# A Mamba-and-router layer on one core: conv halo on GpSimd, carries of two slots in one copy, router and last norm in other slots

## The chip, the core and the metric

The kernel runs on one NeuronCore of a Trainium2 chip. The metric is device time in microseconds (us) of one execution; every kernel has an interval from several. The engines are TensorE (PE; its weight loads are PEld), VectorE (DVE), ScalarE (ACT), GpSimd (POOL) and SyncE (SP), which issues every DMA.

## What is computed

Two blocks in a row on `x` of 2 x 2048 tokens, 512 wide, all float32. The first is a Mamba block, the second a router with an expert bias:

```python
x_in = resid_norm @ W_in                          # 1024 channels
conv = depthwise_conv(x_in, conv_w, taps=4)        # causal, along the tokens
x = silu(conv + conv_b)
delta = softplus(x @ W_delta_1 @ W_delta_2 + b_delta_2)
Bm, Cm = x @ W_B, x @ W_C                          # 16 states
h = h * exp(delta * A) + (delta * x) * Bm          # along the tokens, 1024 channels x 16 states
y = sum over states of h * Cm;  y = (y + x * W_D) * silu(skip)
x1 = x0 + layernorm(resid + y @ W_out)
scores = softmax(layernorm(x1) @ router_w + router_b)
out = x1 + layernorm(flat * sum(top8) + top8 @ expert_bias)
```

## The kernel before

The 4096 tokens are 16 chunks of 256 (`T`). A software pipeline runs in **steps** of one chunk each, and a step has 32 **slots** (`SLOTS`). The scan is the backbone: in each slot VectorE runs two `TENSOR_TENSOR_SCAN` instructions of 512 tokens (`scan`, L950), for one state and two tiles of 128 channels. Around it stand:

- ScalarE: `decay` (L707) makes exp(delta * A) for the next slot, and in a **turned** slot `make_ut` (L726) makes the scan's input transposed.
- TensorE: `turn_u` (L1124) transposes that input into the PSUM tile `bank`; it needs the scan of the slot before, since `bank` has one place for each of the two scans. `add_y` (L1129) adds h * C of two slots ago to `y_sum`.
- GpSimd: `weigh` (L612) makes h * C (`hc`) of the slot before. In the ten **plain** slots (`PLAIN_SLOTS`) `make_u` (L596) makes the scan's input for two slots on, and ScalarE writes the exponential to `bank`.

Each engine has its program written out by hand: for step and slot, first the scan's work, then what the jobs of neighbouring chunks have at that slot. The jobs are `norm` (chunk i+3), `prep` (i+2: projection, convolution, delta, B, C), `scan` (i), `gate`, `mix` (i-2: skip, output projection) and `route` (i-3: second norm, router, last norm, output). `at(step, slot)` gives each job its own slot number `s`, which runs on into the next step, so s = 40 of `route` is slot 8 of the step after. `due` returns a semaphore value to wait for, or nothing where an earlier wait covers it.

What the change touches, all on VectorE unless said:

- The convolution (L1008), for each pair `p` of channel tiles in the slots `TAPPED[p]` and `TAPPED[p] + 2`, one tile each. ScalarE has written the last tap with the bias to `hv`. VectorE adds the halo to the first 3 columns, then three taps of 253, 254 and 255 columns. Between these it makes the halo for the next chunk: three instructions on 3, 2 and 1 columns into `edge`. Tap and halo instructions alternate, so each halo instruction stands where its tap waits for the one before (`link`).
- `save_carry` (L921): a copy of the last column of the slot's two scans, after the scans of the next slot.
- `route`: the row maximum `nmx` (L1072, s = 32), the top 8 (L1082 to L1089, s = 34), `o` (L1098, s = 38 and 40), and `moments(o)` (L925 and L928, s = 40). POOL makes the scale of the last norm at s = 42 and the sum x1 + o (L683) at s = 45. SP stores `o` at s = 47, in its single queue of DMAs.

```python
                                    if s in (TAPPED[p], TAPPED[p] + 2):
...
                                        for k in range(TAPS - 1):
                                            reach = TAPS - 1 - k
                                            part = halo[:, 0:reach]
                                            done = weighed(part, got[:, T - reach:], k, part if k else bias_over(reach))
                                            if k == TAPS - 2:
                                                done.then_inc(edge_ready.sem, 1)
                                            last = weighed(row[:, reach:], got[:, 0:T - reach], k, row[:, reach:])
```

## Time and profile before

| | |
|---|---|
| median of 3 executions | 2269.61 us (2267.01 to 2277.3) |
| the profiled execution | 2263.58 us, its span 2261.6 us |
| busy: PE, DVE, ACT, POOL | 85%, 79%, 76%, 81% of the span |
| TensorE's granted clock, mean | 0.953 of full speed |

The span counts from the first instruction to the last. Scans start at 120.6 us and end at 2108.6 us; in between are 16 steps. The first three take 116 to 125 us, the eleven after them 127 to 131 us each, and the rest is the pipeline's filling and draining. "Busy" is the time in which an engine runs an instruction, waits left out. A step that the text below calls "the shown step" is the one whose first scan starts at 1120.7 us and whose successor's starts at 1248.6 us.

### The profile page before, as it was taken

The numbers are of one execution on the slowest core, as the hardware profiler recorded it, in microseconds if no ns is written. First come the engines' busy times: TensorE is split into PE (matmuls) and PEld (weight loads), VectorE is DVE, ScalarE is ACT, GpSimd is POOL, SyncE is SP. The second block draws the span as 40 slices with busy tenths as digits, with TensorE's granted clock in tenths as the row PEclk, the third lists the DMA queues.
The fourth block names the chain that finished last, engine by engine and source line by source line (L and its number), as shares of the span: only waits on it lengthen the run. The fifth ranks groups of instructions, "written<-read, shape, count | busy, mean of one in ns | idle before, by whom it ended". The sixth has DMA issues, their size and how long they took to land. (4 is left out here: it accounts for less than half of the span.)

```text
span 2261.6 us, 36229 instructions
## 1 busy us (share of the span) xinstructions
PE 1914.7 (85%) x12005; PEld 1602.1 (71%) x12005; DVE 1796.8 (79%) x3105; ACT 1716.9 (76%) x3404; POOL 1840.5 (81%) x1160
## 2 busy tenths in 40 slices
PE   5677777988889898898989898898989989888883
PEld 4567676868778687877778686877768686767551
DVE  3478878798898988898888888889888988888422
ACT  2479797887879796987879797887979788888321
POOL 1278889797989898998979898898989899999412
PEclk9889899999999999999999999999999999999996
DMA  5556566665747576665747566564757556554320
GB/s 162 186 183 201 171 188 223 211 221 174 228 144 268 174 226 203 220 206 173 234 157 263 168 200 235 194 226 147 246 173 241 170 164 231 179 182 159 118 69 19
DMA packets 234676, 425.96 MB, mean 188 GB/s; under 512 B 18622, under 2 KB 134906, under 8 KB 234490
## 3 DMA queue, kind: packets, MB, share of 16 engines
q1 hardware_dynamic: 234490, 423.65, 57.6%
q8 instruction: 96, 1.57, 0.3%
q14 instruction: 90, 0.74, 0.1%
HBM read 339.18 MB, written 84.41 MB: 187 GB/s over the span
## 5 line engine op out<-in xcount | busy, mean ns | idle before, releaser
L612 POOL TENSOR_TENSOR hc<-h,c_all 128x1024 f32<-128x1024 f32 x512 | 1206.1, 2367 | 183.9 <-DVE h L950 169.8
L950 DVE TENSOR_TENSOR_SCAN h<-operand,carry,bank 128x512 f32<-128x512 f32 x528 | 658.7, 1272 | 152.1 <-PE bank L1124 121.4
L726 ACT ACTIVATE u_t<-dx_t,lbc 128x256 f32<-128x256 f32 x1408 | 632.2, 498 | 62.7 <-PE bank L1124 62.7
L1124 PE MATMUL bank<-ident,u_t 128*128 128x128 f32 x2816 | 450.4, 285 | 228.4 <-DVE h L950 214.7
L1129 PE MATMUL y_sum<-ident,hc 128*128 128x128 f32 x4096 | 604.4, 279 | 4.7 <-POOL hc L612 4.3
L1124 PEld LDWEIGHTS bank<-ident,u_t 128*128 128x128 f32 x2816 | 343.0, 146 | 367.7 <-issue 241.4
L1129 PEld LDWEIGHTS y_sum<-ident,hc 128*128 128x128 f32 x4096 | 494.2, 145 | 47.6 <-issue 36.0
L707 ACT ACTIVATE operand<-delta_q,neg_a 128x512 f32<-128x512 f32 x704 | 479.8, 711 | 0.0
L707 ACT ACTIVATE bank<-delta_q,neg_a 128x512 f32<-128x512 f32 x320 | 218.5, 683 | 260.4 <-DVE h L950 259.8
L596 POOL TENSOR_TENSOR operand<-dx_q,b_all 128x1024 f32<-128x1024 f32 x160 | 378.8, 2367 | 8.7 <-DMA b_all<-bc_dram 8.4
L950 DVE TENSOR_TENSOR_SCAN h<-bank,carry,operand 128x512 f32<-128x512 f32 x240 | 294.9, 1269 | 11.8 <-POOL operand L596 7.4
L1335 PE MATMUL mixed<-wout,ys 128*128 128x512 f32 x512 | 264.3, 605 | 3.5 <-DVE ys L1044 3.5
L1255 PE MATMUL pair_bank<-rnt,win 128*128 128x256 f32 x1024 | 251.3, 392 | 11.9 <-DVE x L988 8.4
L950 DVE TENSOR_TENSOR_SCAN h<-operand,bank 128x512 f32<-128x512 f32 x176 | 210.3, 1213 | 59.4 <-PE bank L1124 44.8
L1309 PE MATMUL routed<-rnt_gate,wskip 128*128 128x256 f32 x1024 | 245.5, 385 | 11.2 <-DVE thg L1032 8.7
L1255 PEld LDWEIGHTS pair_bank<-rnt,win 128*128 128x128 f32 x1024 | 195.2, 198 | 49.2 <-issue 21.5
L1309 PEld LDWEIGHTS routed<-rnt_gate,wskip 128*128 128x128 f32 x1024 | 190.2, 193 | 36.7 <-issue 9.8
L1008 DVE SCALAR_TENSOR_TENSOR hv<-pair_bank,taps,hv 128x253 f32<-128x253 f32 (+2 forms) x384 | 181.5, 473 | 0.0
L646 POOL TENSOR_TENSOR dx<-delta,x 128x1024 f32<-128x1024 f32 x32 | 75.8, 2371 | 61.0 <-ACT delta L817 61.0
L1335 PEld LDWEIGHTS mixed<-wout,ys 128*128 128x128 f32 x512 | 79.3, 192 | 36.9 <-issue 32.8
L950 DVE TENSOR_TENSOR_SCAN h<-bank,operand 128x512 f32<-128x512 f32 x80 | 94.1, 1210 | 9.0 <-ACT bank L707 7.3
L1266 PE MATMUL pair_bank<-wlbc,x 128*128 128x160 f32 x512 | 92.2, 330 | 6.7 <-DVE x L988 6.7
(115 smaller groups left out, 1963.6 us busy)
## 6 DMA issues: line engine op xcount, KB each, us to landing
c_all<-bc_dram SPq DMA_DIRECT2D x256, 512.0 KB, 4.3
b_all<-bc_dram SPq DMA_DIRECT2D x160, 256.0 KB, 5.5
win<-in_L_attn_W_in SPq DMA_DIRECT2D x64, 512.0 KB, 5.7
wskip<-in_L_attn_W_skip SPq DMA_DIRECT2D x64, 512.0 KB, 6.7
x_dram<-x SPq DMA_DIRECT2D x64, 256.0 KB, 6.3
delta_dram<-delta SPq DMA_DIRECT2D x32, 512.0 KB, 7.5
dx_dram<-dx SPq DMA_DIRECT2D x32, 512.0 KB, 5.4
delta_q<-delta_dram SPq DMA_DIRECT2D x32, 512.0 KB, 6.6
```

The lines of the kernel that those rows point to most:

```text
L596: nc.gpsimd.tensor_tensor(operand[:, number % 3], dx_q[:, k], b_all[:, j % 2:j % 2 + 1].to_broadcast([P, 2, SPAN]), ALU.mult).then_inc(u_r ...
L612: nc.gpsimd.tensor_tensor(hc[:, number % 3], h[:, number % 3], c_all[:, j % 2, s % 2:s % 2 + 1].to_broadcast([P, 2, SPAN]), ALU.mult).then ...
L707: nc.scalar.activation(to, delta_q[:, k, q], ACT.Exp, scale=neg_a[:, et, n:n + 1]).then_inc(exp_ready.sem, 1)
L726: last = nc.scalar.activation(u_t[:, j % 2, b], dx_t[:, k, b], ACT.Copy, scale=lbc[:, stage % 2, b, DELTA + n:DELTA + n + 1])
L950: nc.vector.tensor_tensor_scan(h[:, number % 3, q], first, second, start, ALU.mult, ALU.add).then_inc(scan_done.sem, 1)
L1008: return nc.vector.scalar_tensor_tensor(out=to, in0=of, scalar=taps[:, et, k:k + 1], in1=onto, op0=ALU.mult, op1=ALU.add)
L1124: last = transpose(bank[:, q, b * P:(b + 1) * P], u_t[:, j % 2, b, q * P:(q + 1) * P], ident[:])
L1129: return matmul(to, lhsT=of, rhs=ident[:], is_transpose=True, start=start, stop=stop, skip_group_check=True)
L1255: last = matmul(pair_bank(p)[:, e * T:(e + 1) * T], win[:, p % 2, k, e * P:(e + 1) * P], rnt[:, k, :], start=(k == 0), stop=(k == KD - 1))
L1266: last = matmul(pair_banks[0][:, b * LBC:(b + 1) * LBC], x[:, et, b * P:(b + 1) * P], wlbc[:, et, :], start=(et == 0 and b == 0), stop=(et ...
L1309: last = matmul(routed[:, e * T:(e + 1) * T], wskip[:, p % 2, k, e * P:(e + 1) * P], rnt_gate[:, k, :], start=(k == 0), stop=(k == KD - 1))
L1335: last = matmul(mixed[:], ys[:, et, b * P:(b + 1) * P], wout[:, et, :], start=(et == 0), stop=(et == ET - 1))
```

## The change

It does five things:

- VectorE no longer makes the halo. At the second tile of a pair it copies the last three inputs of both tiles to `tail` (one instruction, `tail_ready`). At s = 21 of `prep` GpSimd makes the halo of all 8 tiles in six instructions, each linked to the one before (`edge_ready`, now once a chunk).
- `save_carries` runs in even slots only and copies the carries of two slots in one instruction; the tile `carry` is laid out so that it can.
- The second tile's taps have slots of their own, `TAPPED_NEXT`: pair 1 goes from slot 3 to slot 2.
- `route` moves: nmx from s = 32 to 33, exp and top 8 from 34 to 35, the transposition of the weights from 35 (late in the slot) to 36 (early), the bias matmuls from 37 and 39 (late) to 38 and 40 (early), `o` from 38 and 40 to 39 and 41, `moments(o)` from 40 to 43, POOL's scale from 42 to 45, ScalarE's norm from 44 to 47, POOL's sum from 45 to 48 and SP's store from 47 to 50.
- Slot 16 is plain in place of slot 18.

```diff
-PLAIN_SLOTS = (0, 2, 4, 7, 10, 13, 18, 22, 25, 29)
+PLAIN_SLOTS = (0, 2, 4, 7, 10, 13, 16, 22, 25, 29)
 TAPPED = (-5, 1, 6, 10)
+TAPPED_NEXT = (-3, 2, 8, 12)
...
-        carry = sb("carry", P, N, ET)
+        carry = sb("carry", P, N // 2, 2, ET)
...
-                            if "route" in jobs_now and s == 47:
+                            if "route" in jobs_now and s == 50:
...
+                                if s == 21:
+                                    if v := due(pool, tail_ready, t, PAIRS):
+                                        pool.wait_ge(tail_ready.sem, v)
+                                    if v := due(pool, conv_done, t, ET):
+                                        pool.wait_ge(conv_done.sem, v)
+                                    width = TAPS - 1
...
+                                    link(times(edge[:], tail[:], tap(0, width)))
+                                    link(nc.gpsimd.tensor_tensor(edge[:], edge[:],
+                                                                 cbias[:].unsqueeze(2).to_broadcast([P, ET, width]),
+                                                                 ALU.add))
+                                    link(times(tail[:, :, 0:1], tail[:, :, 2:3], tap(2, 1)))
+                                    link(times(tail[:, :, 1:3], tail[:, :, 1:3], tap(1, 2)))
+                                    link(nc.gpsimd.tensor_tensor(edge[:, :, 0:2], edge[:, :, 0:2], tail[:, :, 1:3],
+                                                                 ALU.add))
+                                    last = nc.gpsimd.tensor_tensor(edge[:, :, 0:1], edge[:, :, 0:1], tail[:, :, 0:1],
+                                                                   ALU.add)
+                                    last.then_inc(edge_ready.sem, 1)
...
-                    if v := due(dve, carry_saved, t, s - 1):
+                    if v := due(dve, carry_saved, t, (s - 1) // 2):
...
-                    if v := due(dve, scan_done, t, 2 * (s + 1)):
+                    if v := due(dve, scan_done, t, 2 * (s + 2)):
                         dve.wait_ge(scan_done.sem, v)
-                    copied(carry[:, n, 2 * quarter:2 * quarter + 2],
-                           h[:, number % 3, :, SPAN - 1]).then_inc(carry_saved.sem, 1)
+                    first = number % 3
+                    both = h[:, 0:3:2] if first == 2 else h[:, first:first + 2]
+                    copied(carry[:, n // 2, :, 2 * quarter:2 * quarter + 2],
+                           both[:, :, :, SPAN - 1]).then_inc(carry_saved.sem, 1)
...
-                        save_carry(step, slot - 1)
+                        if slot % 2 == 0:
+                            save_carries(step, slot - 2)
...
-                                    if s in (TAPPED[p], TAPPED[p] + 2):
+                                    if s in (TAPPED[p], TAPPED_NEXT[p]):
...
+                                        if e:
+                                            pair = pair_bank(p).rearrange("p (e t) -> p e t", e=2)
+                                            copied(tail[:, 2 * p:2 * p + 2], pair[:, :, T - width:]).then_inc(
+                                                tail_ready.sem, 1)
                                         for k in range(TAPS - 1):
                                             reach = TAPS - 1 - k
-                                            part = halo[:, 0:reach]
-                                            done = weighed(part, got[:, T - reach:], k, part if k else bias_over(reach))
-                                            if k == TAPS - 2:
-                                                done.then_inc(edge_ready.sem, 1)
...
-                                if s == 32:
+                                if s == 33:
...
-                                if s in (38, 40):
-                                    b = (s - 38) // 2
+                                if s in (39, 41):
+                                    b = (s - 39) // 2
...
-                                if s == 40:
+                                if s == 43:
                                     if v := due(dve, o_ready, t, TB):
                                         dve.wait_ge(o_ready.sem, v)
                                     moments(o, mvo, var_o)
```

VectorE's order in slot 8 of a full step, before (line L950 is the two scans of a slot, L1008 the taps and the halo):

```order
L950 SCALAR_TENSOR_TENSOR h<-operand,carry,bank 128x512 x2
L921 TENSOR_REDUCE carry<-h 128x2
L1098 SCALAR_TENSOR_TENSOR o<-h,stats,routed 128x512
L925 BN_STATS stat<-o 128x6 x2
L928 BN_AGGR mvo<-stat 128x2 x2
L1008 SCALAR_TENSOR_TENSOR hv<-pair_bank,taps,edge 128x3
L1008 SCALAR_TENSOR_TENSOR edge<-pair_bank,taps,cbias 128x3
L1008 SCALAR_TENSOR_TENSOR hv<-pair_bank,taps,hv 128x253
L1008 SCALAR_TENSOR_TENSOR edge<-pair_bank,taps,edge 128x2
L1008 SCALAR_TENSOR_TENSOR hv<-pair_bank,taps,hv 128x254
L1008 SCALAR_TENSOR_TENSOR edge<-pair_bank,taps,edge 128x1
L1008 SCALAR_TENSOR_TENSOR hv<-pair_bank,taps,hv 128x255
```

Slot 8 and slot 9 of the same step now (L972 is the scans, L1035 the taps, L1127 is `o`):

```order
L972 SCALAR_TENSOR_TENSOR h<-operand,carry,bank 128x512 x2
L943 TENSOR_REDUCE carry<-h 128x2x2
L1035 SCALAR_TENSOR_TENSOR hv<-pair_bank,taps,edge 128x3
L943 TENSOR_REDUCE tail<-pair_bank 128x6
L1035 SCALAR_TENSOR_TENSOR hv<-pair_bank,taps,hv 128x253
L1035 SCALAR_TENSOR_TENSOR hv<-pair_bank,taps,hv 128x254
L1035 SCALAR_TENSOR_TENSOR hv<-pair_bank,taps,hv 128x255
L972 SCALAR_TENSOR_TENSOR h<-operand,carry,bank 128x512 x2
L1082 TENSOR_TENSOR z<-mixed,z 128x512
L1127 SCALAR_TENSOR_TENSOR o<-h,stats,routed 128x512
```

The halo's three instructions and the moments of `o` have left slot 8, and the second half of `o` now stands in slot 9 behind `z`.

GpSimd's order from slot 20 to slot 22, before:

```order
L596 TENSOR_TENSOR operand<-dx_q,b_all 128x1024
L612 TENSOR_TENSOR hc<-h,c_all 128x1024 x2
L646 TENSOR_TENSOR dx<-delta,x 128x1024
L574 TENSOR_SCALAR stats<-mvh 128x2
L575 TENSOR_TENSOR stats<-stats,mhalf 128x2
```

and now:

```order
L598 TENSOR_TENSOR operand<-dx_q,b_all 128x1024
L614 TENSOR_TENSOR hc<-h,c_all 128x1024
L572 TENSOR_TENSOR edge<-tail,taps 128x24
L651 TENSOR_TENSOR edge<-edge,cbias 128x24
L572 TENSOR_TENSOR tail<-tail,taps 128x8
L572 TENSOR_TENSOR tail<-tail,taps 128x8x2
L656 TENSOR_TENSOR edge<-edge,tail 128x8x2
L658 TENSOR_TENSOR edge<-edge,tail 128x8
L614 TENSOR_TENSOR hc<-h,c_all 128x1024
L668 TENSOR_TENSOR dx<-delta,x 128x1024
```

Six small instructions stand between the products of slots 20 and 21.

## Rows read from the trace of the kernel before

**Rows 1.** The page, part 1: busy time, share of the span, instructions.

```profile
PE 1914.7 (85%) x12005; PEld 1602.1 (71%) x12005; DVE 1796.8 (79%) x3105; ACT 1716.9 (76%) x3404; POOL 1840.5 (81%) x1160
```

**Rows 2.** Windows: length, busy us of PE, PEld, DVE, ACT, POOL, clock, DMA.

```profile
1120.00:1248.60 128.60, 117.50 (x757) 99.35 (x756) 109.97 (x197) 107.61 (x214) 113.14 (x71) 0.97 0.62 203
...
1152.90:1161.90 9.00, 9.00 (x51) 6.89 (x52) 8.57 (x18) 2.03 (x5) 6.98 (x3) 1.00 0.53 181
...
1178.80:1209.50 30.70, 30.68 (x222) 28.89 (x223) 25.23 (x37) 27.93 (x58) 28.42 (x16) 1.00 0.71 253
```

**Rows 3.** Waits of the whole span: engine, line, whom; us, times, longest.

```profile
PE bank L1124 <- DVE h L950: 214.7, 134, 5.4
POOL hc L612 <- DVE h L950: 169.8, 125, 3.3
DVE h L950 <- PE bank L1124: 166.1, 187, 2.5
...
PEld y_sum L1129 <- POOL hc L612: 7.3, 11, 1.8
```

**Rows 4.** Timeline of VectorE, slots 6 to 8 of one step: start us, us.

```profile
1016.05 0.74 DVE L1098 SCALAR_TENSOR_TENSOR o<-h,stats,routed 128x512 f32<-128x512 f32 x1
1016.70 0.22 DVE L1008 SCALAR_TENSOR_TENSOR hv<-pair_bank,taps,edge 128x3 f32<-128x3 f32 x1
1016.96 0.22 DVE L1008 SCALAR_TENSOR_TENSOR edge<-pair_bank,taps,cbias 128x3 f32<-128x3 f32 x1
1017.10 0.47 DVE L1008 SCALAR_TENSOR_TENSOR hv<-pair_bank,taps,hv 128x253 f32<-128x253 f32 x1
...
1021.14 0.13 DVE L921 TENSOR_REDUCE carry<-h 128x2 f32<-128x2 f32 x1
1021.35 2.45 DVE L950 TENSOR_TENSOR_SCAN h<-operand,carry,bank 128x512 f32<-128x512 f32 x2
...
1024.54 1.29 DVE L925 BATCH_NORM_STATS2 stat<-o 128x6 f32<-128x512 f32 x2
...
1028.07 2.56 DVE L950 TENSOR_TENSOR_SCAN h<-operand,carry,bank 128x512 f32<-128x512 f32 x2
```

**Rows 5.** Groups by form on VectorE: busy us, mean ns, idle before.

```profile
L921 DVE TENSOR_REDUCE carry<-h 128x2 f32<-128x2 f32 x512 | 66.5, 130 | 0.0
...
L1008 DVE SCALAR_TENSOR_TENSOR edge<-pair_bank,taps,cbias 128x3 f32<-128x3 f32 x128 | 28.3, 221 | 4.5
...
L1008 DVE SCALAR_TENSOR_TENSOR edge<-pair_bank,taps,edge 128x1 f32<-128x1 f32 x128 | 28.0, 218 | 4.5
```

**Rows 6.** Timeline of VectorE, slots 0 and 12 of the shown step.

```profile
1125.23 0.29 DVE L1072 TENSOR_REDUCE stats<-routed 128x2 f32<-128x128 f32 x1 [2.15 <-PE routed L1211]
...
1174.21 1.22 DVE L950 TENSOR_TENSOR_SCAN h<-operand,bank 128x512 f32<-128x512 f32 x1 [1.75 <-PE bank L1124]
```

**Rows 7.** Groups by form on GpSimd: its small instructions.

```profile
L575 POOL TENSOR_TENSOR stats<-stats,mhalf 128x2 f32<-128x2 f32 x64 | 45.3, 708 | 5.3
...
L570 POOL TENSOR_TENSOR stats<-stats 128x2 f32<-128x2 f32 x80 | 15.6, 195 | 6.5
```

**Rows 8.** Timeline of GpSimd, slots 14 to 23 of the shown step.

```profile
1183.65 2.37 POOL L612 TENSOR_TENSOR hc<-h,c_all 128x1024 f32<-128x1024 f32 x1 [1.12 <-DVE h L950]
...
1188.45 2.37 POOL L612 TENSOR_TENSOR hc<-h,c_all 128x1024 f32<-128x1024 f32 x1 [0.75 <-DVE h L950]
...
1210.89 2.36 POOL L612 TENSOR_TENSOR hc<-h,c_all 128x1024 f32<-128x1024 f32 x1 [1.46 <-DVE h L950]
...
1221.86 2.36 POOL L612 TENSOR_TENSOR hc<-h,c_all 128x1024 f32<-128x1024 f32 x1
```

**Rows 9.** Timeline of TensorE, slot 25 of the shown step.

```profile
1225.37 0.60 PE L1129 MATMUL y_sum<-ident,hc 128*128 128x128 f32 x4
```

**Rows 10.** Timeline of GpSimd in the last steps, behind the last scan.

```profile
2219.40 2.34 POOL L683 TENSOR_TENSOR o<-x,o 128x1024 f32<-128x1024 f32 x1 [1.63 <-ACT o L688]
```

**Rows 11.** Windows, columns as in rows 2: a stretch at half clock.

```profile
1036.50:1043.40 6.90, 5.72 (x25) 5.72 (x26) 4.22 (x5) 4.69 (x9) 5.89 (x3) 0.51 0.23 75
```

More of the change, by code:

```diff
@@ L155, in build @@
         kept = sb("kept", P, KEPT, 4, TB)
-        edge = sb("edge", P, ET, TAPS - 1)
+        edge, tail = sb("edge", P, ET, TAPS - 1), sb("tail", P, ET, TAPS - 1)
         hv = sb("hv", P, 2, 2, T)
@@ L207, in build @@
         ut_turned = signal("ut_turned", "scan", 2 * before(TURNED_SLOTS, SLOTS))
[L208 removed]
+        carry_saved = signal("carry_saved", "scan", SLOTS // 2)
         hc_ready, hc_read = signal("hc_ready", "scan", SLOTS), signal("hc_read", "scan", SLOTS)
@@ L638, in _, with tap @@
                             if "prep" in jobs_now:
+                                if s == 21:
[4 more added lines that the diff above has]
+                                    width = TAPS - 1
+                                    def tap(k, n):
+                                        return taps[:, :, k:k + 1].to_broadcast([P, ET, n])
+                                    link(times(edge[:], tail[:], tap(0, width)))
[9 more added lines that the diff above has]
+                                    last.then_inc(edge_ready.sem, 1)
                                 for eh in range(2):
@@ L948, in scan, with carry_place, save_carries @@
                             first, second = second, first
-                        start = 0.0 if stage % STAGES_PER_BATCH == 0 else carry[:, n, et:et + 1]
+                        start = 0.0 if stage % STAGES_PER_BATCH == 0 else carry[:, n // 2, carry_place(number - 2 * SLOTS), et:et + 1]
                         nc.vector.tensor_tensor_scan(h[:, number % 3, q], first, second, start, ALU.mult,
                                                      ALU.add).then_inc(scan_done.sem, 1)
-                def save_carry(t, s):
+                def carry_place(number):
+                    return number % 2 ^ (number // 2 * 2 % 3 == 2)
+                def save_carries(t, s):
                     if not (now := slot_of(t, s)):
@@ L1059, in _ @@
                                         dve.wait_ge(z_ready.sem, v)
-                                    if v := due(dve, nz_ready, t - 1, 1):
-                                        dve.wait_ge(nz_ready.sem, v)
+                                    for read in (nz_ready, var_o):
+                                        if v := due(dve, read, t - 1, 1):
+                                            dve.wait_ge(read.sem, v)
                                     moments(z, mvz, var_z)
@@ L1212, in side_work @@
                                 last.then_inc(logits_done.sem, 1)
-                            if s == 35 and late:
+                            if s == 36 and not late:
                                 if v := due(pe, w_ready, t, 1):
@@ L1218, in side_work @@
                                 last.then_inc(w_turned.sem, 1)
-                            if s in (37, 39) and late:
-                                b = (s - 37) // 2
+                            if s in (38, 40) and not late:
+                                b = (s - 38) // 2
                                 if v := due(pe, wt_ready, t, 1):
```

33 lines of the change are left out of this document (16 added, 17 removed).

## The prediction

> **What bounds the kernel now.** I read the page first, part 1 for the busy shares [rows 1]: no engine is above 85%, so no engine alone sets the time. Then the windows, to see one full step apart from filling and draining [rows 2]: in 128.6 us TensorE is busy 117.5, GpSimd 113.1, VectorE 110.0 and ScalarE 107.6. Even the fullest has 11 us of idle time a step. The waits tell why [rows 3]: TensorE waits 214.7 us for the scan and the scan waits 166.1 us for TensorE. They take turns. `turn_u` of the next slot can start only when this slot's scan has left its half of `bank`, and the next scan can start only when `turn_u` has filled it. With one buffer between them, a slot with much VectorE work leaves TensorE idle, and a slot with much TensorE work leaves VectorE idle; the step is the sum of the longer of the two, stretch by stretch. So I followed the timelines of the shown step and the one before, backwards from waiter to releaser. Three kinds of stretch came out:
>
> - Slots 13 to 21 are TensorE's: 30.68 us busy of 30.70 [rows 2]. Nothing that VectorE loses there counts.
> - Slots 7 and 8 are held by both: TensorE is busy 9.00 us of 9.00 in the shown step [rows 2]. In the step before, VectorE's own work in the same slots came out longest: its scans start at 1021.35 in slot 8 and at 1028.07 in slot 9, 6.72 us apart with no idle time, since `o`, its moments and a tile's taps all stand in slot 8 [rows 4].
> - Slots 1, 5 to 6, 9 to 10, 12, and one of 27 and 29, are VectorE's: TensorE has run out of work and waits for a scan that stands behind taps.
>
> GpSimd, 113 us busy, is less tight than it looks: TensorE's loads for `y_sum` wait for its product 7.3 us in the whole span [rows 3], while it waits 169.8 us for scans.
>
> **The halo leaves VectorE.** Per step 24 instructions of 218 to 221 ns [rows 5], 5.3 us of busy time. On the engine's path each is worth less: the halo instruction starts at 1016.96 and the tap behind it at 1017.10, 0.14 us later [rows 4], as they overlap. Without it the tap would start 0.04 us behind the 3-column one's end, where the halo did. So 0.14 x 3 = 0.42 us a tile. Of the eight tiles a step five stand in VectorE's stretches: 2.1 us. The other three are covered by TensorE's stretches of slots 2 to 4, 7 to 8 and by ScalarE's and TensorE's work in 27 to 29; if that cover were gone they'd be worth another 1.3. The added copy to `tail`, four a step, is like the carry's: 130 ns busy [rows 5], some 0.04 on the path when more work follows. Two of the four lie in VectorE's stretches: 0.1 back. Halo: -2.0 us a step.
>
> **Carries.** 16 of 32 copies go, 2.1 us busy. Where nothing follows but the next scan, a copy costs 0.21 us (1021.14 to 1021.35 [rows 4]), as the scan waits for it; behind it, work overlaps and it costs 0.04. In VectorE's stretches some four copies go, mostly of the second sort: -0.2 us a step.
>
> **Moves.** `o` (0.65 us on the path [rows 4]) leaves slot 6, in VectorE's stretch, and its other half enters slot 9, in VectorE's stretch too: 0. nmx (0.29 us) enters slot 1: +0.3; it sat in slot 0 after a wait of 2.15 us for TensorE's logits [rows 6], and `turn_u` stands behind these in the same queue, so leaving slot 0 gains nothing. `moments(o)`, 1.5 us, leaves slot 8 for slot 11. In slot 8 TensorE's 9.0 us take over as the limit, against 9.4 that VectorE took there in the step before: -0.2 on average. In slot 11 it puts off slot 12's first scan, but the second waits 1.75 us for TensorE [rows 6], which is more than the 1.5: 0. The top 8 and pair 1's taps swap slots inside TensorE's stretch: 0. On TensorE the bias matmuls move from late in a slot to early in the next, within one stretch: 0. Slot 16 plain for slot 18 takes four pairs of transpositions from slot 15 and puts them in slot 17, both in the 30.7 us stretch: 0. SP's store waits in its queue three slots later for a sum that GpSimd also makes three slots later: 0. Sum of the moves: +0.1.
>
> **GpSimd.** The six halo instructions resemble its 195 ns ones [rows 7]. With 24 columns at most for 2 I take 0.24 for the widest and 0.08 between linked ones: 1.8 us a step. The lower bound is 1.2 (195 ns each, no gap), the upper 4.7 (708 ns each [rows 7]). Its work for the last norm, 2.3 us, also moves from slot 10, where it had idle time, into slot 13. Together 4.1 us come into slots 13 to 21, which hold idle 1.12 + 0.75 + 1.46 = 3.3 us [rows 8]. So the product of slot 21 comes 0.8 us later. Next in line is TensorE's `add_y`: it starts at 1225.37 on a product that ends at 1224.22 [rows 8, 9], 1.15 us of slack, the smallest I found in the step. 0.8 fits: cost 0.
>
> The Trainium skill (GPSIMD Engine Reference, 3.1) keeps elementwise work on the Vector engine, giving 4497 ns against 2293 for the same addition, a rule that speaks against this part. By it, halo work moved one for one would cost GpSimd twice 5.3 us a step and lose. The rows don't bear that out at this size: 195 ns [rows 7] against 218 [rows 5], and 24 instructions become six.
>
> **Sum.** A full step: -2.0 - 0.2 + 0.1 = -2.1 us; eleven of them, -23. Three earlier steps without all jobs, and the two chunks prepared ahead of the first scan: about -1.6 each, -8. Draining: the sum x1 + o, 2.34 us [rows 10], used to stand ahead of the next chunk's norm on GpSimd; now that norm's scale comes first, -2, but z is ahead of `o` and puts the latter off, 0.7 in each of three steps: 0. That is -31. Where VectorE gives way, TensorE and ScalarE are next, and I take a quarter off for it: **-24 us**. From the profiled 2263.6 (span 2261.6 and 2.0 around it) that makes 2239.6; the median of the runs shown is 6.0 above the profiled one, so the forecast is 2245.6, say **2246**. Without the quarter off: 2239; with GpSimd's and ScalarE's work taking back half: 2254.
>
> **Rivals.** *More than that.* TensorE's clock falls to half where it idled behind VectorE's stretch: in the step of rows 4 the granted clock was 0.51 (the 1.2 GHz level, of 1.2 and 2.4) for 6.9 us after slots 9 and 10, and TensorE was busy 5.72 of them [rows 11]; at full clock that work would take half, 2.9 us less. The shown step's mean is 0.97 [rows 2], so 6% of it, 7.7 us, ran at half. If shorter stretches of VectorE end most of that, and half of it is on the path, 1.9 a step, another -21: 2225. The Trainium skill (TensorE: Matmul & The Clock Gate, Part 1) says that idleness throttles and activity releases; by it slot 8's relief would help. Against it: slots 9 to 11 keep about as much VectorE work as before, and now have `o` and its moments in them.
>
> *No change.* The stretches swap owners: TensorE is busy 117.5 of 128.6, so ScalarE or TensorE stands just behind VectorE in each slot, and what is taken off in slots 5 to 10 is waited for in 7 to 8. Then -5 or so: 2264.
>
> *Slower.* GpSimd becomes the limit in slots 21 to 31. It decides from the point where its six instructions and the moved norm outgrow 3.3 us of idle time plus 1.15 of slack. At 4.7 for the six it is 4.7 + 2.3 - 4.45 = 2.6 us late at `add_y`, each step; with the 2.1 gained and in the steps without `route` less, +0.5 to +1 a step, and what it delays (the next step's slots 0 to 3, where it catches up) up to as much again: 2285. For it: it has no idle time from 1188.45 to 1209.4 [rows 8]. Against it: rows of 195 ns.
>
> *It doesn't do what it says*: the carry copy could wait for a second scan and hold up the next one in even slots. It stands behind the same scans as before, so I give that nothing of its own.
>
> **Chances.** Forecast 0.50, more 0.18, no change 0.20, slower 0.12. A measurement can tell about 0.5%, 11 us, from no change. Faster by over 0.5%: 0.68; within: 0.20; slower: 0.12. The range takes in the clock rival and the carried-over bounds, down to 2210, and the no-change case up to 2274.
>
> **What would show it.** Right: a full step of 126 to 127 us in place of 128.6; VectorE's busy time down by some 90 us (84.5 of halo, half of 66.5 [rows 5] of carries, less the copies) while TensorE's wait for scans falls by 20 to 30; in slot 8 no idle time of TensorE; GpSimd's six instructions near 0.2 us each. Wrong: GpSimd instructions of 0.4 us or more and waits of `y_sum` for `hc`; or TensorE's stretches at half clock gone, and steps under 125 us; or a step as long as before with VectorE's idle time grown by what it lost.

## The result, and the profile after

| | before | after |
|---|---|---|
| median | 2268.31 us (2264.78 to 2277.3, 4 runs) | 2230.49 us (2229.44 to 2231.7, 4 runs) |
| ratio | | **0.9845 [0.9821, 0.9869]** |
| the profiled execution | 2263.58 us, span 2261.6 | 2231.22 us, span 2229.4 |

The change makes the kernel 35 to 38 us faster. The forecast was 2246 us in a range of 2210 to 2274: the measured time lies on its side and in its range, 15 us below it. Busy times, in part 1 of the page after (before: [rows 1]):

```profile
PE 1907.9 (86%) x12005; PEld 1592.3 (71%) x12005; DVE 1733.4 (78%) x2529; ACT 1717.0 (77%) x3404; POOL 1861.0 (83%) x1256
```

VectorE has lost 63 us and 576 instructions, GpSimd has gained 20.5 us and 96. The prediction said some 90 for VectorE, and its own terms would make more: it added up single instructions (84.5 us of halo), and the page counts time in which two overlap only once. The groups by form after, line, engine, operation, count, then busy us and mean ns, answer to [rows 5]:

```profile
L943 DVE TENSOR_REDUCE carry<-h 128x4 f32<-128x4 f32 x256 | 34.3, 134 | 0.0
L943 DVE TENSOR_REDUCE tail<-pair_bank 128x6 f32<-128x6 f32 x64 | 10.6, 165 | 2.2
L572 POOL TENSOR_TENSOR edge<-tail,taps 128x24 f32<-128x24 f32 x16 | 3.7, 232 | 38.2 <-DVE hv L1035 38.2
...
L658 POOL TENSOR_TENSOR edge<-edge,tail 128x8 f32<-128x8 f32 x16 | 3.4, 212 | 1.3
```

The carry copy costs the same for four columns as for two, and the six instructions on GpSimd take 212 to 232 ns each.

The waits of the whole span after (us, times, longest) answer to [rows 3]:

```profile
ACT bank L729 <- DVE h L972: 289.4, 163, 4.4
DVE h L972 <- PE bank L1153: 211.1, 188, 2.9
PE bank L1153 <- DVE h L972: 184.7, 127, 5.1
POOL hc L614 <- DVE h L972: 125.7, 97, 2.7
DVE h L972 <- ACT operand L729: 36.4, 57, 1.4
...
PE routed L1207 <- DVE o L1127: 17.4, 12, 1.5
PEld y_sum L1158 <- POOL hc L614: 14.6, 27, 2.2
```

TensorE waits 30 us less for scans, but the scan waits 45 us more for TensorE. VectorE gave up 63 us of work and the span fell by 32: half of the work came back as waiting. With the halo alone (e1, below) VectorE gave up 44.6 us and the span fell by 43.6: nothing of it came back.

**Where the 32 us are.** The starts of the scans in the two timelines cut the span. The first scan starts at 120.6 us before and at 113.7 after (-6.9). The first three steps take 358.7 and 350.7 (-8.0), the eleven after them 1412.8 and 1397.0 (-15.8, which is -1.4 each), step 14 109.3 and 108.6 (-0.7), and the rest 260.3 and 259.4 (-0.9).

Inside a step I cut at slot boundaries and average ten full steps, the fourth to the thirteenth. This is the yardstick of the experiments (us per step; all columns are experiments told of below):

| slots | before | after | e1 halo alone | e3 moves alone | e5 plain slot alone | e6 | e7 | e9 |
|---|---|---|---|---|---|---|---|---|
| 0 to 4 | 20.54 | 19.37 | 19.26 | 20.74 | 20.39 | 18.97 | 19.23 | 19.24 |
| 5 to 7 | 11.86 | 11.33 | 11.54 | 11.89 | 11.85 | 11.33 | 11.32 | 11.90 |
| 8, 9 | 9.85 | 9.87 | 9.70 | 10.00 | 9.84 | 9.87 | 9.89 | 8.53 |
| 10 to 13 | 17.54 | 16.67 | 16.48 | 17.75 | 17.94 | 16.85 | 16.24 | 16.56 |
| 14 to 22 | 33.58 | 35.10 | 33.59 | 34.65 | 34.31 | 33.84 | 33.67 | 33.67 |
| 23 to 31 | 35.19 | 34.74 | 35.32 | 35.09 | 34.90 | 37.37 | 34.84 | 34.68 |
| step | 128.55 | 127.08 | 125.88 | 130.11 | 129.23 | 128.22 | 125.19 | 124.58 |

Two things stand out after. Slots 8 and 9, whose two lumps of VectorE the change pulled apart, are as long as before. And slots 14 to 22, where I had costed the edits at nothing, are 1.5 us longer: that stretch took back half of the 3.0 us that the others gained. Windows of one full step after and of those slots in it (length, busy us of PE, PEld, DVE, ACT, POOL, clock), for [rows 2]:

```profile
1224.50:1352.90 128.40, 116.14 (x749) 97.65 (x748) 105.11 (x159) 106.50 (x213) 118.79 (x82) 0.97 0.61 208
...
1281.29:1311.75 30.46, 30.22 (x219) 28.03 (x217) 23.62 (x31) 28.73 (x57) 29.77 (x21) 1.00 0.65 223
1290.40:1311.00 20.60, 20.60 (x150) 19.16 (x149) 16.23 (x22) 20.55 (x42) 20.44 (x12) 1.00 0.85 289
```

In the last window three engines are full at once: TensorE 20.60 of 20.60 us, ScalarE 20.55, GpSimd 20.44. "TensorE is busy 30.68 of 30.70" [rows 2] was true and not the whole of it. Nor does a busy TensorE have no room: with slot 16 plain alone (e5) its busy time in slots 14 to 22 grew from 32.4 to 32.9 us a step with nearly the same number of matmuls (233.5 and 234.2), at the full clock in both.

### The profile page after: what moved, and what is told of

Read it like the earlier page. It is cut to its first block and busy times, and to the rows that moved or that the text cites. A ratio compares the mean times of both kernels' runs of the same rounds, so it can differ in the third digit from the quotient of the medians.

```text
span 2229.4 us, 35466 instructions
## 1 busy us (share of the span) xinstructions
PE 1907.9 (86%) x12005; PEld 1592.3 (71%) x12005; DVE 1733.4 (78%) x2529; ACT 1717.0 (77%) x3404; POOL 1861.0 (83%) x1256
## 5 line engine op out<-in xcount | busy, mean ns | idle before, releaser
L972 DVE TENSOR_TENSOR_SCAN h<-operand,carry,bank 128x512 f32<-128x512 f32 x528 | 659.4, 1271 | 190.5 <-PE bank L1153 160.5
L1153 PE MATMUL bank<-ident,u_t 128*128 128x128 f32 x2816 | 445.8, 283 | 186.9 <-DVE h L972 184.7
L972 DVE TENSOR_TENSOR_SCAN h<-bank,carry,operand 128x512 f32<-128x512 f32 x240 | 295.4, 1268 | 15.4 <-POOL operand L598 6.8
L972 DVE TENSOR_TENSOR_SCAN h<-operand,bank 128x512 f32<-128x512 f32 x176 | 209.8, 1212 | 65.5 <-PE bank L1153 50.5
L1035 DVE SCALAR_TENSOR_TENSOR hv<-pair_bank,taps,hv 128x253 f32<-128x253 f32 (+2 forms) x384 | 184.5, 480 | 11.4
L972 DVE TENSOR_TENSOR_SCAN h<-bank,operand 128x512 f32<-128x512 f32 x80 | 94.0, 1209 | 13.3 <-ACT bank L729 8.7
L1295 PEld LDWEIGHTS pair_bank<-wlbc,x 128*128 128x128 f32 x512 | 82.4, 214 | 7.3 <-DVE x L1018 7.3
```

The lines of the kernel that those rows point to most:

```text
L972: nc.vector.tensor_tensor_scan(h[:, number % 3, q], first, second, start, ALU.mult, ALU.add).then_inc(scan_done.sem, 1)
L1035: return nc.vector.scalar_tensor_tensor(out=to, in0=of, scalar=taps[:, et, k:k + 1], in1=onto, op0=ALU.mult, op1=ALU.add)
L1153: last = transpose(bank[:, q, b * P:(b + 1) * P], u_t[:, j % 2, b, q * P:(q + 1) * P], ident[:])
L1295: last = matmul(pair_banks[0][:, b * LBC:(b + 1) * LBC], x[:, et, b * P:(b + 1) * P], wlbc[:, et, :], start=(et == 0 and b == 0), stop=(et ...
```

## The experiments

### One part of the change at a time

**Halo alone**, on the kernel before:

```diff
+                                if s == 21:
...
+                                    link(times(edge[:], tail[:], tap(0, width)))
...
+                                        if e:
...
+                                            copied(tail[:, 2 * p:2 * p + 2], pair[:, :, T - width:]).then_inc(
...
-                                            part = halo[:, 0:reach]
-                                            done = weighed(part, got[:, T - reach:], k, part if k else bias_over(reach))
```

> Before, with the halo alone moved to GpSimd (slots of all jobs as before, a copy of the carry in every slot). Theory A (the halo's time on VectorE's path is the gain): the first scan starts some 7 us earlier, as it does in the changed kernel (16 tiles ahead of it at 0.42 us), and the whole is 22 to 30 us faster, two thirds or more of the change's 35. Theory B (the moves are the gain, since slot 8 with its two lumps of VectorE is what starves the others): 7 to 12 us faster, nearly all of it ahead of the first scan.

Measured: 2217.61 us, ratio 0.9788 [0.976, 0.9815]. The halo alone is worth some 48 us, more than the whole change and far more than either theory allowed.

**Carries alone** (`carry` laid out by pairs of slots, and this):

```diff
-                        save_carry(step, slot - 1)
+                        if slot % 2 == 0:
+                            save_carries(step, slot - 2)
```

> Before, with the carries of two slots in one copy and nothing else. Theory A: 3 to 6 us faster (0.2 us a step on the path, up to 0.4 where slots hold nothing but scans). Theory B: under 2 us.

Measured: 2262.72 us, ratio 0.9984 [0.996, 1.0008]. Nothing that can be told from no change.

**Moves alone** (the slots of `route`, pair 1's second tile, and slot 16 plain for 18; neither halo nor carries):

```diff
-PLAIN_SLOTS = (0, 2, 4, 7, 10, 13, 18, 22, 25, 29)
+PLAIN_SLOTS = (0, 2, 4, 7, 10, 13, 16, 22, 25, 29)
+TAPPED_NEXT = (-3, 2, 8, 12)
...
-                                if s in (38, 40):
-                                    b = (s - 38) // 2
+                                if s in (39, 41):
+                                    b = (s - 39) // 2
...
-                                if s == 40:
+                                if s == 43:
```

> Before, with the moves alone: route's slots, pair 1's second tile from slot 3 to 2, slot 16 plain for 18. Halo and carries as before. Theory A: within 5 us of before, since slots 8 and 9 take as long together as before and o enters slot 9, VectorE's own. Theory B: 15 to 25 us faster.

Measured: 2276.21 us, ratio 1.0054 [1.0037, 1.0072]. The moves cost 12 us, which neither theory had. TensorE's busy time rose with the same number of instructions, and with the halo alone it fell. First the page of the moves alone, then that of the halo alone:

```profile
PE 1933.0 (85%) x12005; PEld 1611.6 (71%) x12005; DVE 1793.7 (79%) x3105; ACT 1717.3 (76%) x3404; POOL 1840.1 (81%) x1160
```

```profile
PE 1894.8 (85%) x12005; PEld 1585.8 (71%) x12005; DVE 1752.2 (79%) x2785; ACT 1717.1 (77%) x3404; POOL 1859.4 (84%) x1256
```

The same 12005 matmuls take 38 us more in one than in the other, and most of that is the clock. TensorE was busy at the 1.2 GHz level for 192.9 us with the moves alone and for 131.0 with the halo alone; half of the difference is 31 us. That is the clock of the prediction's first rival, seen in TensorE's busy time. How much of it reaches the kernel's time is another question, since not all of it is on the path.

**The changed kernel with the halo back on VectorE** (the first diff reversed, on the kernel after):

```diff
-                                if s == 21:
...
+                                            part = halo[:, 0:reach]
+                                            done = weighed(part, got[:, T - reach:], k, part if k else bias_over(reach))
```

> The changed kernel with the halo back on VectorE. Theory A: it loses 22 to 30 us of the change's 35 and is 5 to 13 us faster than before. Theory B: it loses 7 to 12 us and is 23 to 28 us faster than before.

Measured: 2264.52 us, ratio 0.9994 [0.9974, 1.0013]. Without the halo the rest of the change is worth nothing; the halo carries all of the 35 us, again more than theory A had.

### Slots 14 to 22: which move costs

**Slot 16 plain for slot 18**, alone on the kernel before:

```diff
-PLAIN_SLOTS = (0, 2, 4, 7, 10, 13, 18, 22, 25, 29)
+PLAIN_SLOTS = (0, 2, 4, 7, 10, 13, 16, 22, 25, 29)
```

> Before, with slot 16 plain in place of slot 18 and nothing else. Theory C (ScalarE is a limit in slots 15 to 22: a plain slot spares it four products u_t, and in slot 16 it also makes it wait for the scan before): slots 14 to 22 take 1.0 to 1.5 us longer, 12 to 20 us in all, all that the moves alone lost or more. Theory D (the loss of the moves lies in route: GpSimd's norm and ScalarE's norm of o, now in slots 13 and 15): within 4 us of before.

Measured: 2273.8 us, ratio 1.0049 [1.0029, 1.0069], as much as all the moves together, though less than theory C's 12 to 20 us. The waits give the reason. ScalarE's timeline in slots 15 and 16 of a full step, start and us, of the kernel after:

```profile
1286.03 0.69 ACT L729 ACTIVATE bank<-delta_q,neg_a 128x512 f32<-128x512 f32 x1 [0.70 <-DVE h L972]
1286.65 0.89 ACT L748 ACTIVATE u_t<-dx_t,lbc 128x256 f32<-128x256 f32 x2
1288.54 0.69 ACT L729 ACTIVATE bank<-delta_q,neg_a 128x512 f32<-128x512 f32 x1 [0.99 <-DVE h L972]
```

and VectorE's timeline in slots 18 and 19 of the same step:

```profile
1295.80 1.22 DVE L972 TENSOR_TENSOR_SCAN h<-operand,bank 128x512 f32<-128x512 f32 x1 [1.39 <-ACT operand L729]
...
1299.70 2.47 DVE L972 TENSOR_TENSOR_SCAN h<-operand,bank 128x512 f32<-128x512 f32 x2 [0.80 <-ACT operand L729]
```

In a plain slot ScalarE writes its exponential into `bank`, so it must wait for the scan there (0.70 and 0.99 us); in a turned slot it writes to `operand` and runs ahead. Behind these waits it runs without a gap until 1311, as it did before: its idle time in slots 18 to 22 averages 0.05 us in both kernels. Slot 18, turned now, adds two pairs of `u_t` (0.9 us each) there. So the lead is lost, the load has grown, and the scans of slots 18 and 19 wait 1.39 and 0.80 us. The kernel with slot 16 plain alone shows the first part by itself: ScalarE's idle time in slots 14 to 17 is 3.39 us a step in it and 2.15 before.

**The changed kernel with slot 18 plain again:**

```diff
-PLAIN_SLOTS = (0, 2, 4, 7, 10, 13, 16, 22, 25, 29)
+PLAIN_SLOTS = (0, 2, 4, 7, 10, 13, 18, 22, 25, 29)
```

> The changed kernel with slot 18 plain again. Theory C: 12 to 20 us faster than the changed kernel, ratio to before 0.976 to 0.979; slots 14 to 22 back at 33.6 us. Theory D: within 4 us of the changed kernel, 0.984.

Measured: 2249.79 us, ratio 0.9935 [0.9916, 0.9954]. It is slower than the change. Slots 14 to 22 came back to 33.84 us, so ScalarE's norm of `o`, which is still moved here, isn't what cost them; but slots 23 to 31 grew from 34.74 to 37.37. The waits of this kernel:

```profile
PEld pair_bank L1207 <- DMA dx_q<-dx_dram: 34.7, 8, 6.9
...
PEld y_sum L1158 <- POOL hc L614: 32.3, 49, 2.2
DVE h L972 <- POOL operand L598: 23.2, 22, 2.4
PE y_sum L1158 <- POOL hc L614: 17.2, 21, 2.0
```

and its timeline of slots 24 and 25:

```profile
1328.86 2.35 POOL L614 TENSOR_TENSOR hc<-h,c_all 128x1024 f32<-128x1024 f32 x1
...
1331.16 2.37 POOL L598 TENSOR_TENSOR operand<-dx_q,b_all 128x1024 f32<-128x1024 f32 x1
1331.27 0.86 PEld L1158 LDWEIGHTS y_sum<-ident,hc 128*128 128x128 f32 x8 [1.23 <-POOL hc L614]
...
1333.74 2.34 DVE L972 TENSOR_TENSOR_SCAN h<-bank,operand 128x512 f32<-128x512 f32 x2 [1.04 <-POOL operand L598]
```

In the kernel after, the same place reads (the first four of the twelve loads are for the product before):

```profile
1318.29 2.35 POOL L614 TENSOR_TENSOR hc<-h,c_all 128x1024 f32<-128x1024 f32 x1
...
1320.60 2.37 POOL L598 TENSOR_TENSOR operand<-dx_q,b_all 128x1024 f32<-128x1024 f32 x1
1321.29 1.34 PEld L1158 LDWEIGHTS y_sum<-ident,hc 128*128 128x128 f32 x12
```

Here GpSimd is the limit. Its product ends, TensorE's load starts at once and has waited 1.23 us for it, and behind it the scan waits 1.04 us for `operand`. That is the mechanism of my "slower" rival. Averaged over the fifth to the fourteenth step, the product that TensorE needs in slot 24 is ready 1.50 us ahead before, 1.51 in the change and 0.05 in this kernel. Of the 2.6 us, slot 24 has 1.05. Slot 29 has another 1.12: there in every second step TensorE waits for `dx_q`, a transfer of what GpSimd makes in slots 22 to 26, for 2.9 to 4.2 us, where in the change it is 1.8 to 2.7. That is the first line of these waits, 34.7 us in all against 23.0 in the change. With slot 16 plain GpSimd makes one scan input two slots earlier, where it still has idle time. So the two moves pay for each other: the last norm, moved to where GpSimd has no slack left, needs slot 16 plain, and slot 16 plain costs ScalarE's lead.

**Halo and carries without any move**, on the kernel before:

```diff
+                                if s == 21:
...
+                        if slot % 2 == 0:
+                            save_carries(step, slot - 2)
```

> Before, with halo and carries changed and none of the moves. If parts add up: ratio 0.9788 x 0.9984 = 0.977, 52 us faster than before and 17 faster than the changed kernel. If the carries are hidden once the halo is gone: 0.979.

Measured: 2215.7 us, ratio 0.979 [0.977, 0.9809]: 12 to 15 us faster than the whole change. Slots 14 to 22 take 33.67 us and slots 23 to 31 34.84. Without the moves there is no collision. The ratio is that of the halo alone: the carries add nothing to it.

### Slots 8 and 9: what holds them

The forecast had both VectorE and TensorE as holders of these slots. The next two kernels move TensorE's work, the first of them nothing else. **In the changed kernel with slot 18 plain, the second bias matmul (1.1 us) goes from slot 8 to slot 9:**

```diff
-                            if s in (38, 40) and not late:
-                                b = (s - 38) // 2
+                            if s in (38, 41) and not late:
+                                b = (s - 38) // 3
```

> The changed kernel with slot 18 plain again and the second bias matmul of route moved on TensorE from slot 8 to slot 9 (o's second half stays in slot 9). If TensorE's 9 us of work set the length of slots 7 to 9 (theory A), its 1.05 us leave that stretch: slots 8 and 9 together take 8.8 to 9.3 us in place of 9.9, 8 to 13 us in all against the changed kernel with slot 18 plain. If VectorE sets it with z and o in slot 9, nothing is won, since o then waits for the matmul.

Measured: 2238.11 us, ratio 0.9882 [0.9863, 0.9901], 12 us faster than its parent e6. Slots 8 and 9 went from 9.87 to 8.84 us. There TensorE was the limit, and there VectorE's split had gained nothing. The matmul found room in slot 9 because the change had made some: with the second half of `o` behind `z`, TensorE waits for `o` there. In the kernel after:

```profile
1264.91 0.63 PE L1207 MATMUL routed<-ident,dx_q 128*128 128x128 f32 x4 [1.40 <-DVE o L1127]
```

This wait is 17.4 us in the whole run of the change and of e6, and 4.1 in e8.

**On e7, the second bias matmul one slot earlier, and `o` behind it:**

```diff
-                                if s in (38, 40):
-                                    b = (s - 38) // 2
+                                if s in (38, 39):
+                                    b = s - 38
...
-                            if s in (37, 39) and late:
-                                b = (s - 37) // 2
+                            if s in (37, 38) and late:
+                                b = s - 37
```

> Halo and carries changed, route in its old slots but for two: the second bias matmul goes on TensorE from slot 7 to the end of slot 6, where TensorE waited 1.4 us for a scan, and the second half of o from slot 8 to slot 7, which held nothing but scans. GpSimd, ScalarE and SP as in e7. Theory A: TensorE's stretch of slots 7 to 9 loses 1.05 us, but VectorE, with the moments of o and a tile's taps in slot 8, lets go only 0.4 to 0.6 of it: 5 to 8 us faster than e7, ratio 0.975 to 0.977. Rival: VectorE's stretch is the limit whole, then within 2 us of e7.

Measured: **2200.25 us, ratio 0.9709 [0.9692, 0.9726]**, the best of all: 30 us under the change, 66 under the kernel before and 15 to 18 under e7, where 5 to 8 had been expected. Slots 8 and 9 take 8.53 us in place of 9.89, slots 5 to 7 0.58 more and slots 10 to 13 0.32 more; the full step is 0.61 shorter. Both halves of `o` now stand ahead of slot 8's taps, and TensorE has one job fewer between slot 8's scans and slot 9's; this kernel doesn't tell the two apart. The clock is not what gained it: in the ten steps 37.5 us run at 1.2 GHz, against 23.9 in e7. The eleven full steps make 7 of the 15 us between the profiled executions. Of the rest, 3.4 lie behind the last scan's start and 2.2 in the last step of scans, and no run shows why. VectorE's scans of slots 8, 9 and 10 in e7:

```profile
1242.19 2.31 DVE L971 TENSOR_TENSOR_SCAN h<-operand,bank 128x512 f32<-128x512 f32 x2
...
1248.51 1.21 DVE L971 TENSOR_TENSOR_SCAN h<-operand,bank 128x512 f32<-128x512 f32 x1
...
1252.12 1.21 DVE L971 TENSOR_TENSOR_SCAN h<-bank,operand 128x512 f32<-128x512 f32 x1
```

and in e9:

```profile
1239.83 2.32 DVE L971 TENSOR_TENSOR_SCAN h<-operand,bank 128x512 f32<-128x512 f32 x2
...
1245.32 2.32 DVE L971 TENSOR_TENSOR_SCAN h<-operand,bank 128x512 f32<-128x512 f32 x2
...
1248.14 1.22 DVE L971 TENSOR_TENSOR_SCAN h<-bank,operand 128x512 f32<-128x512 f32 x1
```

The two distances were 6.32 and 3.61 us and are 5.49 and 2.82.

**e9 with the moments of `o` in slot 11**, as the change has them, and what follows later by two slots:

```diff
-                                if s == 40:
+                                if s == 43:
...
-                                if s == 42:
+                                if s == 44:
...
-                                if s == 45:
+                                if s == 47:
```

> As e9, with the moments of o in slot 11, GpSimd's norm in slot 12, ScalarE's in slot 14, GpSimd's sum in slot 15 and the store in slot 17. Theory A alone: slots 7 to 9 take 1.0 us less than in e7, 12 us in all, ratio 0.972 to 0.974. With theory E (GpSimd's work must not come later than in the kernel before, since its slack at TensorE's y_sum in slots 24 and 25 is 1.1 us and the halo has taken of it): slots 23 to 31 grow by 1 us or more, and it is no faster than e7 or slower, 0.979 to 0.99.

Measured: 2231.55 us, ratio 0.9845 [0.9827, 0.9863], 31 us slower than e9. Slots 8 and 9 fell further, to 8.16, but slots 23 to 31 rose by 1.9 to 36.61, and TensorE's product in slot 24 was ready only 0.21 us ahead (1.24 in e9). The split of the two lumps gains 0.4 us and costs 1.9, on GpSimd, thirteen slots later. The whole step is 1.9 longer, which is 21 of the 31 us; the rest lies in the first steps and behind the last scan.

### GpSimd's slack, measured

**On e7, twelve more small instructions on GpSimd** at slot 21; nobody reads what they write:

```diff
+        spare = sb("spare", P, 4, TAPS)
...
+                                    for _ in range(12):
+                                        link(times(spare[:], taps[:, 0:4], taps[:, 4:8]))
```

> e7 with twelve more small linked instructions on GpSimd behind the six of the halo (16 columns each, their result is read by nobody), some 0.3 us each, 3.6 us a step. Theory E (the slack at y_sum is 1.1 us): TensorE waits for hc in slots 23 to 31, 2 to 2.5 us a step, 25 to 35 us slower than e7, ratio 0.990 to 0.995. Rival (GpSimd is hidden behind TensorE and ScalarE there): at most 5 us slower, 0.981.

Measured: 2264.91 us, ratio 0.9992 [0.9974, 1.0011]. The group of the twelve (16 times), and the waits:

```profile
L572 POOL TENSOR_TENSOR spare<-taps 128x16 f32<-128x16 f32 x192 | 42.6, 222 | 13.8
```

```profile
PEld y_sum L1159 <- POOL hc L614: 56.5, 50, 2.6
DVE h L974 <- POOL operand L598: 48.3, 26, 3.7
PE y_sum L1159 <- POOL hc L614: 41.7, 31, 2.3
```

Busy and gaps make 3.5 us a step, and slots 23 to 31 grew by 3.55 us, from 34.84 to 38.39. That the two are alike is chance. In e7 the product for slot 24 is ready 1.24 us ahead, the halo not having used that up, and 3.5 less this slack is 2.3; slot 24 grew by 2.43. The other 1.1 us stand behind it, in slots 26, 29 and 31 (0.44, 0.48 and 0.34). There stretches at 1.2 GHz now begin in slot 24, 17.1 us of them in ten steps where e7 has none, and the wait for `dx_q` is longer again. So the expectation had the slack and the first wait right (2 to 2.5 us), and what follows from them was missing: 46 to 49 us lost against e7 where it said 25 to 35.

**e9 with the halo at slot 14 in place of 21**, where GpSimd also had idle time [rows 8]:

```diff
-                                if s == 21:
+                                if s == 14:
```

> The kernel of e9_bias6_simple (halo on GpSimd, one carry copy in two slots, a bias matmul earlier), with GpSimd's six halo instructions at slot 14 in place of slot 21, and nothing else changed. The six take 1.8 us. Theory (GpSimd's idle time has to be in the right slots): the trace of before showed idle time of 1.12 and 0.75 us in slots 14 and 15 and 1.46 us in slot 21; the 1.8 us at slot 14 are covered by the first two, so that slots 22 to 31 start with a GpSimd 0.4 us earlier; stretch 14 to 22 stays at 33.7 us, stretch 23 to 31 falls by up to 0.4 us from 34.68, TensorE's waits of y_sum for hc fall below 13.0, and the ratio to before is 0.967 to 0.971. Rival (the six instructions at slot 21 are wholly covered already, by slack of 0.84 to 1.24 us in front of y_sum): the ratio stays within 0.0015 of 0.9709 and both stretches stay as they are. Second rival (work that GpSimd does in slots 14 and 15 puts off hc there, and TensorE, which has no idle time in that stretch, waits): stretch 14 to 22 grows by 0.5 us or more, ratio above 0.974.

Measured: 2201.21 us, ratio 0.9714 [0.9698, 0.9731], the same as e9. GpSimd's idle time moved (slots 14 to 17 from 1.64 us to 0.81, slots 18 to 22 from 0.39 to 1.26) and nobody used it; TensorE's loads for `y_sum` wait 13.0 us for `hc` in both. Six instructions at slot 21 are covered. Slots 23 to 31 did fall by 0.18 us, to 34.50, but the full step is 0.18 longer and the time is the same: the theory that the six cost something where they stand falls.

## Why the prediction was right, and where it was wrong

**Kind and place of the gain: right.** It is VectorE's path, given back by the halo, and the carries are worth next to nothing (e1, e2, e4). Of what was to show it, a full step of 126 to 127 us (127.08) and TensorE's waits for scans down by 20 to 30 us (30) came out, and VectorE's 90 us didn't (63).

**0.42 us a tile: nearly.** Ahead of the first scan nothing else stands between tiles. Two tiles' 3-column instructions there start 2.07 us apart before and 1.70 after:

```profile
108.74 0.22 DVE L1008 SCALAR_TENSOR_TENSOR hv<-pair_bank,taps,edge 128x3 f32<-128x3 f32 x1 [7.56 <-ACT hv L688]
...
110.81 0.21 DVE L1008 SCALAR_TENSOR_TENSOR hv<-pair_bank,taps,edge 128x3 f32<-128x3 f32 x1
```

```profile
101.58 0.22 DVE L1035 SCALAR_TENSOR_TENSOR hv<-pair_bank,taps,edge 128x3 f32<-128x3 f32 x1 [6.76 <-ACT hv L710]
...
103.28 0.21 DVE L1035 SCALAR_TENSOR_TENSOR hv<-pair_bank,taps,edge 128x3 f32<-128x3 f32 x1
...
103.60 1.51 DVE L1035 SCALAR_TENSOR_TENSOR hv<-pair_bank,taps,hv 128x253 f32<-128x253 f32 x3
```

That is 0.37 for a tile without the copy; the second tile, from its first instruction to its last tap's end, went from 2.14 to 1.83 with the copy in it, 0.31.

**"Of the eight tiles a step five stand in VectorE's stretches: 2.1 us": too small, by a tile's place and by the size of two slots.** With the halo alone, slots 1, 6, 10 and 12 are shorter by 0.38, 0.39, 0.38 and 0.63 us, but so is slot 3, by 0.67, which I had called covered by TensorE. Slot 8's 0.44 come back as 0.28 in slot 9, and slot 27's 0.38 as 0.48 in slot 29. The full step lost 2.67 us, against the 2.0 predicted. The excess stands in slots 3 and 12, and the clock was there. Windows of slots 1 to 4 of a full step, before and then with the halo alone (behind the five busy times stands the granted clock, 0.90 and 1.00):

```profile
866.66:883.04 16.38, 14.26 (x84) 11.67 (x83) 14.94 (x36) 12.25 (x28) 13.57 (x7) 0.90 0.89 283
```

```profile
847.75:862.27 14.52, 12.77 (x86) 10.19 (x85) 14.15 (x30) 11.15 (x26) 11.54 (x6) 1.00 0.88 279
```

Over ten full steps, before, the 1.2 GHz level fills 17.1 us that begin in slot 2 and 30.7 in slot 11; with the halo alone none in slot 2, and 20.5 in slots 11 and 12. In slot 29, which grew, it went the other way, from 3.4 to 13.7. All slots together it is 54.6 us before, 34.1 with the halo alone, 44.4 in the change and 81.9 with the moves alone. Work at half clock that runs at full takes half the time, so 20.5 us less in ten steps are worth up to 1.0 us a step. That fits the excess of 0.7; it is a bound from rows, and I have no run that separates it. The rival "more than that" was thus probably part of the truth, in slots 3 and 12, and with the moves half of it went again (slots 10 and 13 in the change: 20.5 us where before and e7 have none). What TensorE did before its clock fell: in slots 1 and 2 it was idle for 2.1 us a step before and 1.7 with the halo alone, in slots 10 and 11 for 4.3 and 3.9. The Trainium skill (TensorE: Matmul & The Clock Gate, Part 1) has idleness throttle the engine and activity release it. These four figures agree with that. e9 does not fit so simply: TensorE is idle for 3.6 us there and 34.1 us at 1.2 GHz begin in slots 10 to 12, where e7 has 3.9 and 17.0.

**Head and first steps: too small by half.** "About -1.6 each, -8" came out as -14.9: -6.9 ahead of the first scan and -8.0 in three steps. In the head all 16 tiles of two chunks are on the path, at 0.31 to 0.37 each 5.4 us; I had priced two chunks like two steps with their covers. What the other 1.5 us are isn't shown. The head has less 1.2 GHz after (17.1 us, 30.7 before), but with the halo alone it has more of it than the change, and the first scan still starts earlier, at 113.0. Nor is it shown why the first three steps gave 8.0 us where 5 were due; kernels with the halo on VectorE vary there between 355.2 and 358.7 us.

**"Slot 16 plain for slot 18 ...: 0": wrong, the failed step of the full steps.** It costs 0.7 us a step alone, of the 1.56 that the moves cost together where the sum had 0.1, and, by the difference of e6 and the change, 1.3 in slots 14 to 22 of the changed kernel. I read one engine of that window as full and took it for the only limit. Its neighbour in the row, ScalarE with 27.93 of 30.70 [rows 2], is full from the middle on, and only the timeline shows that.

**"Cost 0" on GpSimd: right for the halo, wrong for the company it keeps.** The prices were right: 1.8 us for the six, predicted from the 195 ns rows, where the upper bound of 708 ns each was far off. e12 shows the halo hidden. But with the norm of `o` behind it the slack of 1.15 us was gone (e6: 0.05 us left, and slots 23 to 31 2.5 us longer than in e7), and the change escaped only because slot 16 was plain. I had summed 4.1 us of work against 3.3 of idle time and 1.15 of slack and stopped there. The slack itself was read rightly, 1.50 us in slot 24 and 1.08 in slot 25 on average. What didn't hold was the idle time set against the work: e7 has 0.39 us of it left in slots 18 to 22, the change 0.51, and idle time in slots before the last norm's sum can't take up what comes behind it.

The rule of the Trainium skill (GPSIMD Engine Reference, 3.1), elementwise work on the Vector engine, would have kept the halo there and lost 48 us. On this size the rows have GpSimd at 212 to 232 ns against VectorE's 218 to 221, and batching made 24 instructions six.

**"`moments(o)` ... leaves slot 8 for slot 11: -0.2" and nmx: wrong in detail.** Slots 8 and 9 did not move at all (9.85 and 9.87): TensorE's bias matmul, output projection and two tiles of input projection hold them. VectorE then waits for TensorE in slot 9, as the timeline after shows:

```profile
1258.72 1.12 PE L1254 MATMUL routed<-ebias,low 64*128 64x512 f32 x2
...
1262.31 1.22 DVE L972 TENSOR_TENSOR_SCAN h<-operand,bank 128x512 f32<-128x512 f32 x1 [2.32 <-PE bank L1153]
```

nmx's wait for the logits fell (36.3 us to 16.8), but the scan's wait for TensorE grew by 45 us: the wait changed its owner.

**The quarter off: wrong, and the sum under it was right by luck.** Undiscounted, the sum was -31 against -32.4 between the profiled executions, and it came so close because two errors cancel: head and first steps 7 too small, eleven full steps 7 too large. The full steps in turn hide two more, the halo too small and the moves too cheap. The discount for "the next limit" was laid on terms that already had their covers taken out. It made 7.0 of the 15 us (a quarter of 31 leaves 23; the prediction wrote 24). Another 6.7 is the offset: I added 6.0 for median over profiled execution, and the profiled execution after is 0.7 above its median. The remaining 1.4 is the sum's.

**What stays open.** How much of the halo's 2.67 us is clock. What shortened the head and the first steps beyond the taps. And why the halo is worth 48 us on the kernel before and 34 in the changed one: the sum of the parts alone, -48 - 4 + 12, is -40 where the change has -35. The table puts that difference into slots 14 to 22 (+1.5 in the change, +1.1 with the moves alone), no further.

## What to carry to other kernels

A window in which one engine is full says only that this engine is a limit. Before an edit in it is costed at nothing, every other engine's longest run without a gap in it has to be read from its timeline. Where work is handed to an engine that is off the path, note for each waiter how far ahead its input is ready, and spend that slack only once: two additions that each fit can together be a microsecond late in every step, and the first wait brings others behind it. And moving work off the engine that holds a slot can gain nothing until the engine next to it is relieved too; here one bias matmul moved by a slot gave 12 us (e8), and with `o` 15 to 18 (e9), while pulling apart two lumps on VectorE gave none in the change.

## What was unexpected in the hardware

- The clock of TensorE goes with a few tenths of a microsecond of VectorE's work. In ten full steps, stretches at 1.2 GHz that begin in slot 2 fill 13.7 to 20.5 us in the five kernels with the halo on VectorE and none in the nine with it on GpSimd.
- The same 12005 matmuls took 1892 to 1936 us in these kernels. Take half of the time away in which TensorE was busy at 1.2 GHz (124 to 199 us), and 1828 to 1838 us are left in all of them.
- GpSimd's `TENSOR_TENSOR` takes 212 ns on 8 columns and 232 ns on 24, linked ones start 0.3 us apart, and among its small ones only the power instructions take 708 ns [rows 7].
- A small instruction between two dependent ones on VectorE costs less than itself. Two taps of 0.47 us start 0.64 apart with a halo instruction of 0.22 between them, and 0.52 apart without it ((1.51 - 0.48) / 2): 0.13, not 0.22.
